# Where the routed answers of a mixture-of-experts layer are added: after the stage, or sequence by sequence inside the next one

## The reference, cut to what matters

```
x = x + 0.5 * F(layernorm(x))
x = x + G(layernorm(x))
x = x + 0.5 * F(layernorm(x))
return x

def F(u):                       # 2 shared experts, 8 routed experts, top 2
    h_s = sum of both shared experts' MLPs
    gpk, i_topk = top_k(sigmoid(u @ centroids), 2)
    gk = gpk / scores.sum()
    h_r = (gk[..., None] * the two chosen experts' MLPs).sum(-2)
    return u + h_s + h_r

def G(h):                       # per head, a state S carried along the sequence
    S = S * exp(g_t) + k_t v_t ;  o_t = (q_t * scale) . S
    return o @ Wo
```

## Time and profile before

| | us |
|---|---|
| median of 3 runs | 2860.8 |
| the three runs | 2859.31 to 2874.13 |
| the profiled execution, its time | 2870.94 |
| its span, first to last instruction | 2869.2 |

### The profile page before, as it was taken

How to read it: one execution, slowest core, us unless ns; L and a number is a source line. 1 busy time by engine, 2 the same in 40 slices (tenths; PEclk the granted TensorE clock), 3 DMA queues, 4 the chain that set the end, 5 groups by cost and what they waited for, 6 DMA issues and landing times. The chain is left out here.

```text
span 2869.2 us, 51222 instructions
## 1 busy us (share of the span) xinstructions
PE 2330.8 (81%) x14828; PEld 1656.7 (58%) x14828; DVE 2025.6 (71%) x5474; ACT 1377.8 (48%) x2654; POOL 1212.7 (42%) x1060
## 2 busy tenths in 40 slices
PE   5569999999999896778899998088888788898980
PEld 5435455444444554666677776066777676777760
DVE  7666666666666665778777776588888787776664
ACT  4204454455444544666756665032222667666650
POOL 3342211221131132528774555145655387645550
PEclk9759899999998997988999999599999988999995
DMA  2031122121112213401135665500000111356646
GB/s 64 15 45 25 28 34 34 25 35 31 31 28 31 36 24 88 163 34 41 43 122 180 219 218 170 136 1 0 0 0 0 39 41 43 120 200 212 212 161 176
DMA packets 140258, 222.67 MB, mean 78 GB/s; under 512 B 20958, under 2 KB 100624, under 8 KB 129515
## 3 DMA queue, kind: packets, MB, share of 16 engines
q1 hardware_dynamic: 121835, 185.46, 23.6%
q0 software_dynamic: 18176, 34.14, 3.5%
HBM read 136.75 MB, written 57.32 MB: 68 GB/s over the span
## 5 line engine op out<-in xcount | busy, mean ns | idle before, releaser
L950 DVE TENSOR_REDUCE attn_rowmax<-psum 128x1 f32<-128x512 f32 (+3 forms) x748 | 457.8, 637 | 297.4 <-PE psum L788 295.5
L732 ACT ACTIVATE attn_probs<-psum 128x512 f32<-128x512 f32 (+1 forms) x704 | 387.2, 560 | 493.3 <-PE psum L851 484.9
L786 PE MATMUL psum<-attn_ks,attn_qs 72*128 72x512 bf16 (+3 forms) x1088 | 314.5, 325 | 38.2 <-DVE attn_rowmax L950 31.4
L849 PE MATMUL psum<-attn_qs,attn_ks 75*128 75x512 bf16 (+3 forms) x1024 | 290.9, 316 | 36.3 <-issue 25.7
L788 PE MATMUL psum<-attn_mask_qk,attn_ident_b 128*128 128x128 bf16 x1088 | 223.7, 231 | 0.0
L1274 POOL DMA_INDIRECT experts_answers<-ffn1b_y_rows,ffn1b_out_row x156 | 154.4, 990 | 151.3 <-ACT ffn1b_y_rows L1344 111.0
L1274 POOL DMA_INDIRECT experts_answers<-ffn1a_y_rows,ffn1a_out_row x156 | 154.8, 992 | 147.1 <-ACT ffn1a_y_rows L1344 109.3
L849 PEld LDWEIGHTS psum<-attn_qs,attn_ks 75*128 75x128 bf16 x1024 | 101.8, 100 | 193.1 <-ACT attn_probs L732 94.4
L648 POOL TENSOR_TENSOR attn_rstd<-attn_var_eps,minus_half 128x4 f32<-128x4 f32 x18 | 18.3, 1018 | 445.3 <-DVE attn_var_eps L927 445.3
L851 PE MATMUL psum<-attn_mask_kq,attn_ident_b 128*128 128x128 bf16 x1024 | 205.2, 226 | 0.0
L1824 POOL TENSOR_TENSOR gla_state<-gla_state,gla_qT 128x512 f32<-128x512 f32 x128 | 160.0, 1270 | 106.8 <-DVE gla_state L2023 106.8
(11 more groups left out here) (421 smaller groups left out, 6355.4 us busy)
## 6 DMA issues: line engine op xcount, KB each, us to landing
ffn1a_w_ring<-experts_packed SPq DMA_DIRECT2D x39, 1026.5 KB, 5.1
ffn1b_w_ring<-experts_packed SPq DMA_DIRECT2D x39, 1026.5 KB, 5.1
attn_qs<-attn_qparts SPq DMA_DIRECT2D x216, 64.0 KB
attn_ks<-attn_kparts SPq DMA_DIRECT2D x216, 64.0 KB
ffn1a_x_in<-experts_slots SPq DMA_DIRECT2D x39, 264.0 KB, 4.8
ffn1b_x_in<-experts_slots SPq DMA_DIRECT2D x39, 264.0 KB, 4.7
ffn1a_h<-experts_answers SPq DMA_DIRECT2D x16, 512.0 KB, 5.5
ffn1b_h<-experts_answers SPq DMA_DIRECT2D x16, 512.0 KB, 5.4
```

The costliest lines, as they stand in the source:

```text
L732: act.activation(probs[:, j % RING, 0:n], ps_exp[j % 2][:, 0:n], ACT.Exp, scale=SCALE).then_inc(exp_ready, 1)
L786: pe.matmul(out, qs[k][0:K_QK, 4 * g + hh, qt * P:(qt + 1) * P], ks[k][0:K_QK, 4 * g + hh, 0:n_keys], start=True, stop=False)
L849: pe.matmul(out, ks[k][:, 4 * g + hh, kt * P:(kt + 1) * P], qs[k][:, 4 * g + hh, kt * P:N], start=True, stop=False)
L950: dve.tensor_reduce(rowmax[:, NT - 1 - w, h:h + len(heads)], score_bank(n, j)[:, 0:len(heads) * width_of(w)].rearrange("p (a c) -> p a c", ...
```

## The change

The weighing and adding of ffn1a's answers leaves `expert_stage` and goes into `gla_stage`: SP loads the answers of one sequence into one of two buffers (two DMAs of 256 KB), ACT multiplies them by `gk` in place (eight activations), POOL adds the two answers to x (two additions with a drain between them) and counts `x_ready`, and DVE's `layer_norm` waits for it. The first two sequences are done ahead of the loop, sequence s+2 at the beginning of round s; the last round of the loop, which has no sequence to add, is written out behind it on POOL and ACT, with a small memset in place of the addition. `gk` moves into `Experts`, so that it outlives the stage. ffn1b keeps its own passes; after each pass SP issues the loads of the pass after next and then a store of the finished 8 tiles, 512 KB, and `store_stage` goes.

```diff
@@ expert_stage, SP
-                for q in range(TILES // PASS):
-                    if q >= 2:
-                        sp.wait_ge(answers_used, q - 1)
-                    for k in range(2):
-                        at = k * ex.TOKENS + q * PASS * P
-                        sp.dma_start(answers[:, q % 2, k, :, :], ...)
+                if out is not None:
+                    answers_of(0)
+                    answers_of(1)
+                    for q in range(TILES // PASS):
+                        sp.wait_ge(answers_used, q + 1)
+                        if q + 2 < TILES // PASS:
+                            answers_of(q + 2)
+                        sp.dma_start(out_view[:, q * PASS:(q + 1) * PASS, :],
+                                     m.x[:, m.first + q * PASS:m.first + (q + 1) * PASS, :]).then_inc(stored, 16)
+                    sp.wait_ge(stored, 16 * (TILES // PASS))
@@ expert_stage, DVE
-                for q in range(TILES // PASS):
-                    add_answers(q)
+                if out is not None:
+                    for q in range(TILES // PASS):
+                        add_answers(q)
@@ gla_stage, SP, behind the six weight loads
+            for s in range(NB):
+                if s >= 2:
+                    sp.wait_ge(x_ready, s - 1)
+                for k in range(2):
+                    at = k * ex.TOKENS + s * SEQ
+                    sp.dma_start(answers[:, s % 2, k, :, :],
+                                 ex.answers[at:at + SEQ, :].rearrange("(t p) d -> p t d", p=P)
+                                 ).then_inc(answers_in[s % 2], 16)
@@ gla_stage, POOL
+            def add_answers(b, s):
+                pool.wait_ge(weighed, s + 1)
+                x = x_of[:, bass.ds(s * NT + m.first, NT), :]
+                pool.tensor_tensor(x, x, answers[:, b, 0, :, :], ALU.add)
+                pool.drain()
+                pool.tensor_tensor(x, x, answers[:, b, 1, :, :], ALU.add).then_inc(x_ready, 1)
+            # in front of v = 0: add_answers(k, i * 2 + (k + 2)), in the last round a memset of one column
+            add_answers(0, 0)
             inv_std(1)
             pool.memset(state[1][:, :, :], 0.0).then_inc(term_ready, 1)
+            add_answers(1, 1)
             inv_std(2)
             low_part(0, 1)
@@ gla_stage, ACT
+            def weigh_answers(b, s, uses):
+                act.wait_ge(answers_in[b], uses * 32)
+                for k in range(2):
+                    for t in range(NT):
+                        last = act.activation(answers[:, b, k, t:t + 1, :], answers[:, b, k, t:t + 1, :], ACT.Copy,
+                                              scale=ex.gk[:, bass.ds(s * NT + t, 1), k])
+                last.then_inc(weighed, 1)
+            weigh_answers(0, 0, 1)
+            weigh_answers(1, 1, 1)
             turn(0, 1)
+            # in the loop, in front of turn: weigh_answers(k, nxt, i + 2)
@@ gla_stage, DVE
             def layer_norm(tile, count):
+                dve.wait_ge(x_ready, count)
@@ build
-        expert_stage(nc, m, "ffn1b", ex)
-        store_stage(nc, m, out)
+        expert_stage(nc, m, "ffn1b", ex, out)
```

More of the change, by code:

```diff
@@ L73, in __init__ @@
         self.answers = nc.dram_tensor("experts_answers", (2 * self.TOKENS, D), F32, kind="Internal").ap()
+        self.gk = sb("gk", [P, TILES, 2])
         self.cent = sb("cent", [P, self.E_R])
@@ L1046, in attention_stage, with expert_stage @@
         retire(nc, sems)
-def expert_stage(nc, m, name, ex):
+def expert_stage(nc, m, name, ex, out=None):
     G = NT
@@ L1121, in expert_stage @@
         best = sb("best", [P, 2 * G, 2])
-        gk = sb("gk", [P, TILES, 2])
+        gk = ex.gk
         hot = sb("hot", [P, 2, 2 * G, E_R], BF16)
@@ L1182, in expert_stage @@
         answers_used = sem("answers_used")
+        stored = sem("stored")
         ps_h = m.psum[:, 0:C, :]
@@ L1239, in _, with answers_of @@
                 sp.wait_ge(shared_in, 16 * E_S)
-                for q in range(TILES // PASS):
-                    if q >= 2:
-                        sp.wait_ge(answers_used, q - 1)
-                    for k in range(2):
-                        at = k * ex.TOKENS + q * PASS * P
-                        sp.dma_start(answers[:, q % 2, k, :, :],
-                                     ex.answers[at:at + PASS * P, :].rearrange("(t p) d -> p t d", p=P)
-                                     ).then_inc(answers_in[q % 2], 16)
+                if out is not None:
+                    out_view = out.rearrange("b (t p) d -> p (b t) d", p=P)
+                    def answers_of(q):
+                        for k in range(2):
+                            at = k * ex.TOKENS + q * PASS * P
+                            sp.dma_start(answers[:, q % 2, k, :, :],
+                                         ex.answers[at:at + PASS * P, :].rearrange("(t p) d -> p t d", p=P)
+                                         ).then_inc(answers_in[q % 2], 16)
+                    answers_of(0)
[7 more added lines that the diff above has]
+                    sp.wait_ge(stored, 16 * (TILES // PASS))
             @block.gpsimd
@@ L1753, in gla_stage @@
         vT = [sb(f"vT{k}", [P, N]) for k in range(2)]
+        answers = sb("answers", [P, 2, 2, NT, D])
+        idle = sb("idle", [P, 2])
         state = [sb(f"state{k}", [P, TERMS, N]) for k in range(2)]
         weights_in = sem("weights_in")
+        answers_in = [sem(f"answers_in{k}") for k in range(2)]
+        weighed = sem("weighed")
+        x_ready = sem("x_ready")
         var_ready = sem("var_ready")
@@ L1810, in low_part, with sequence @@
                                    ALU.subtract).then_inc(dv_low_ready, 1)
+            def add_answers(b, s):
[4 more added lines that the diff above has]
+                pool.tensor_tensor(x, x, answers[:, b, 1, :, :], ALU.add).then_inc(x_ready, 1)
+            def sequence(i, k, more):
+                for v in range(DH):
+                    if v == 6:
+                        low_part(1 - k, i * 2 + (k + 2))
+                    if v == 0:
+                        if more:
+                            add_answers(k, i * 2 + (k + 2))
+                        else:
+                            pool.memset(idle[:, k:k + 1], 0.0).then_inc(x_ready, 1)
+                    if v == 3:
+                        inv_std(i * 2 + (k + 3))
+                    pool.wait_ge(dv_used, (i * 2 + k) * TERMS + (DV_BANKS + v + 1))
+                    pool.tensor_tensor(state[k][:, v, :], state[k][:, v, :], qT[k][:, :],
+                                       ALU.mult).then_inc(term_ready, 1)
+            add_answers(0, 0)
             inv_std(1)
             pool.memset(state[1][:, :, :], 0.0).then_inc(term_ready, 1)
+            add_answers(1, 1)
             inv_std(2)
             low_part(0, 1)
-            with pool.Fori(0, BODIES) as i:
+            with pool.Fori(0, BODIES - 1) as i:
                 for k in range(2):
[L1818 to L1825, removed]
+                    sequence(i, k, True)
+            for k in range(2):
+                sequence(BODIES - 1, k, False)
         @block.scalar
@@ L1861, in _, with sequence @@
             turn_qp(0, 1)
-            with act.Fori(0, BODIES) as i:
-                for k in range(2):
[L1864 to L1869, removed]
+            def sequence(i, k, more):
+                nxt = i * 2 + (k + 2)
+                if more:
+                    weigh_answers(k, nxt, i + 2)
+                turn(1 - k, nxt)
+                softmax(1 - k, nxt)
+                values(1 - k, nxt, ps_dv[(k * USES + V_USE) % DV_BANKS])
+                high_part(1 - k, nxt)
+                turn_qp(1 - k, nxt)
+            with act.Fori(0, BODIES - 1) as i:
+                for k in range(2):
+                    sequence(i, k, True)
+            for k in range(2):
+                sequence(BODIES - 1, k, False)
         @block.tensor
@@ L2044, in _ @@
             residual(NB)
[L2048 to L2056, removed]
 def build(nc, c, out):
@@ L2078, in build @@
         expert_stage(nc, m, "ffn1a", ex)
[L2079 to L2081 removed]
+        gla_stage(nc, m, "gla", gla, ex)
+        expert_stage(nc, m, "ffn1b", ex, out)
 def layout(inputs):
```

2 lines of the change are left out of this document (1 added, 1 removed).

## The result

| | runs | median us | ratio to before, 95% |
|---|---|---|---|
| before, same comparison | 12 | 2864.68 | |
| after | 12 | 2842.66 (2835.30 to 2854.01) | 0.9926 (0.9903 to 0.9949) |

The change takes 21 us off (0.9926 × 2864.68 = 2843.5; 15 to 28 by the interval; 22.0 between the two medians). The profiled execution after took 2843.61 us (span 2841.7, granted clock 0.904), 27.5 less than the span before.

A forecast was written before the change was run, and what follows sets the result against it. Bounds: serial loads and DVE additions ending ffn1a and ffn1b; DVE from scan 3 to 7 in the loop. Sum -47.1 + 14.2 + 10.5 - 10 = -32.4 us, forecast 2828 us; range 2808 to 2848.

The forecast's parts named there:

- The end of ffn1a: ffn1a's serial loads and DVE additions go, so the scan stage begins at 1806.7 instead of 1853.78: minus 47.1 us.
- The same 3.7 us of block end: Between SP's last wait in ffn1a and the scan stage, block end and clearing were taken to stay 3.7 us.
- The start: Scan stage's first layer norm waits for answer loads, ACT's weighing and POOL's additions: plus 14.2 us, bounds 13 and 17.
- The loop: Scan loop: ten full-clock rounds at 0.85 us, plus one more sequence at the lower clock, 2 us: plus 10.5 us.
- alone: In the loop, the layer norm starting 1.55 to 1.65 us later, without a held var_eps, costs 0 to 0.1 us.
- rival (b): In the loop TensorE's clock falls more often, eight sequences more at 2 us: about 2842 us; chance 0.18.
- The end of ffn1b: Stores issued behind each pass replace the last store stage: minus 10 us, bounds minus 11.6 and minus 7.
- (a): var_eps in the loop isn't held by POOL and the clock stays; loop costs 0 to 2 us, about 2819; chance 0.20.
- the 0.19 us that spoke for (a): DVE's var_eps took 0.19 us beside a busy POOL in the profile before, read as possibly no hold.
- (c): Loads and stores of ffn1b disturb each other and use up the gain of 10 us: about 2838; chance 0.07.
- (d): Slower than before: ACT's weighing beyond 4.36 us delays the xT copy on PE's path, about 2876; chance 0.03.
- the signs named: Timeline checks: first scan 14 us later, var_eps about 1 us, period 21.1 us, five or so slow sequences, eight output DMAs.

The follow-up runs named there:

- e3: Kernel before with only ffn1b's stores issued piece by piece behind each pass, ffn1a's answers added as before: 2853.99 us, ratio 0.9971 to before.
- e2: Changed kernel with the loads of the first two sequences' answers issued ahead of the six weight loads: 2835.01 us, ratio 0.9896 to before.
- e7: Changed kernel with epsilon added on POOL, the first two sequences' answers loaded at ffn1a's end, and extra PE transposes: 2810.96 us, ratio 0.9808 to before.
- e5: Changed kernel with 4, 7 and 2 extra PE transposes in front of scan inputs 0, 1 and 2: 2833.40 us, ratio 0.9885 to before.
- e1: Changed kernel with POOL's two additions and ACT's weighing moved behind the inverse deviation, before v = 3, one sequence earlier: 2834.78 us, ratio 0.9899 to before.
- e4: Changed kernel with epsilon added by POOL in front of its power instead of by DVE's var_eps: 2829.55 us, ratio 0.9860 to before.
- e6: Kernel before with 4, 7 and 2 extra PE transposes in front of scan inputs 0, 1 and 2: 2859.14 us, ratio 0.9977 to before.

## Why the prediction was right, point by point

The time, 2842.66 us, is within the range and 14.7 above the forecast: 3.9 of it because the median before was 2864.68 in this comparison, the rest because the change gave 22.0 between the medians instead of 32.4. Of that the touched stretches explain 5.5 (-26.9); the 5 us left are within the interval, and which of the unprofiled runs had how many slow sequences isn't seen, so they stay open.

**The end of ffn1a, mis-sized by 2.8 us.** "The same 3.7 us of block end" was read where POOL's drain was hidden by 47 us of additions. The cover went, and the drain was next. The forecast asked what SP waits for and not what every engine still does.

**The start, right**: +13.6 for +14.2. The weighing went faster (4.78 us for 16, 0.30 each, against 0.40), the landing was sooner than thought (+7.94 instead of +8.6), and `normalise`, held by the memset and the second sequence's addition, took 5.46 instead of 4.52, inside the bound of 2.7 more.

**The loop, right in mechanism, mis-sized**: +15.3 for +10.5. The price per sequence at full clock was 0.92 for 0.85, out of other parts, so that it came so close is luck: the layer norm starts 1.84 late rather than 1.55 to 1.65 (the gap in front of the second addition was 0.43, not 0.14), its moments take 1.00 instead of 0.84, and the hold is 0.5, not 0.8 to 1.0; with 1.55 of slack, 1.84 + 0.16 + 0.5 - 1.55 = 0.95. The late layer norm "alone" cost not 0 to 0.1 but 0.45 of it (1.84 + 0.16 - 1.55). Eight sequences at 0.92 are 7.4; two more sequences at the lower clock, where one was counted, are 2 × (23.15 - 20.24) = 5.8; the four old ones' lengthening from 22.7 or 23.14 to 23.15 is 0.9, and the first round, up to its scan 3, 1.1 (1854.12 - 1843.63 against 1888.37 - 1879.02). That is 15.2. So rival (b), that the clock falls more often, came true by a quarter: two more, not eight. The Trainium skill, page "TensorE: Matmul & The Clock Gate", part 1, says that the place of the switch varies from run to run. Two pairs of profiles with the same loop agree: before has four sequences at the lower clock, from its third, fourth, eleventh and twelfth scan 3 on, and e3 three, from the first, eighth and ninth; after has six and e2 seven.

**The end of ffn1b, right, and near its bound**: -11.5 for -10, with -11.6 as the bound. In the window above the DMAs moved 294 GB/s, where the forecast had allowed them 262.

**The rivals.** (a), not held, is out: 0.68 us, and without that instruction the price falls by 0.78 (e7 against e5). The trace before could have told. One tile of its division, in a narrow window of the timeline:

```profile
1998.69 1.28 POOL L1824 TENSOR_TENSOR gla_state<-gla_state,gla_qT 128x512 f32<-128x512 f32 x1
1998.75 1.30 DVE L1992 TENSOR_SCALAR gla_qf<-gla_qf,gla_qfinv 128x128 f32<-128x128 f32 x1
```

In each of the 16 sequences the second of the eight tiles takes 1.29 to 1.30 us, where the others take 0.27 to 0.29, and ends 0.08 us behind POOL's multiplication. And `var_eps`, at 0.18 to 0.20 us, ends in each of them 0.02 to 0.03 us behind POOL's v = 1, as it does after: the 0.19 us that spoke for (a) reads as the end of a short hold.

(c) is out: -11.5, and e3 alone -11.7. (d) is out: ACT weighs in 2.44 us and then still waits 2.71 for PE. Of the signs named, the first scan, the wait of the layer norm, scan 3, 21.1 us and eight stores showed as written; `var_eps` was 0.68 rather than 1, and the slow sequences six rather than five.

## What to carry to other kernels

When work that covered the end of a stage is removed, look at every engine's end of that stage, not only at the one that was waited for; work that was put beneath what remains (e7's loads beneath the drain) cost nothing here. Where a POOL instruction is moved, list which DVE instructions will run beside it: moving the meeting (e1) made another DVE instruction wait, removing the DVE instruction gave 0.8 us of each sequence back (e4, and e7 against e5). A tile that takes several times as long as its equals shows in the profile before where such a meeting already is. And before a change of a few us is judged in a loop in which the clock falls now and then, hold the clock still in both kernels, as e5 and e6 do.

## What the runs showed of the hardware

POOL's drain at the end of a stage with indirect DMAs took 9.36 us and ended 4 us past the last of them, in both kernels and both stages. ACT's 128x128 multiplication by a column took 0.30 us (2.44 for eight), against 0.40 in the form that has a bias column too. POOL's addition behind a drain began 0.43 us after the one before had ended in the loop, and 0.13 in the code ahead of it (1815.28 + 1.26 to 1816.67). And thirteen added transposes for each sequence made the loop of the kernel before 9.3 us shorter (346.91 to 337.57): its PE has room for them in its waits. A DVE `tensor_scalar` tile that met a 128x512 instruction of POOL took about 1.3 us instead of 0.28, once in each sequence's division in every kernel.
